# Mixture-of-experts kernel: every slot's rows gathered straight from the conditioned rows, without a table in slot order

## The reference

```python
def _L0_cond_ref(x, W, A, Bm, scalings, adapter_idx):
    H = jnp.einsum('btd,od->bto', x, W)
    xa = jnp.einsum('btd,brd->btr', x, A[adapter_idx])
    delta = jnp.einsum('btr,bor->bto', xa, Bm[adapter_idx])
    return H + delta * scalings[adapter_idx][:, None, None]
...
routing_weights = softmax_integer(xf @ w_gate.T)
top_w, top_i = jax.lax.top_k(routing_weights, 2)
top_w = top_w / top_w.sum(axis=-1, keepdims=True)
combine = jnp.zeros((T, E)).at[jnp.arange(T)[:, None], top_i].add(top_w)
for e in range(8):
    h = jax.nn.silu(xf @ w1[e].T) * (xf @ w3[e].T)
    out = out + combine[:, e:e + 1] * (h @ w2[e].T)
x = x + out
```

## Time and profile before

| | |
|---|---|
| median of 3 runs | 213.94 us |
| the three runs | 209.7, 213.94, 224.81 us |
| profiled execution: span from first to last instruction | 203.8 us |
| profiled execution's own time | not listed beside the runs; the fastest run, 209.7 us, is 5.9 us over the span |
| PE busy | 194.4 us (95%) |
| POOL busy | 134.7 us (66%) |
| DVE, ACT busy | 106.3 us (52%), 82.5 us (40%) |
| DMA traffic | 37.25 MB |

### The profile page before, as it was taken

How to read it: one execution, slowest core, us unless ns; L and a number is a source line. 1 busy time by engine, 2 the same in 40 slices (tenths; PEclk the granted TensorE clock), 3 DMA queues, 4 the chain that set the end, 5 groups by cost and what they waited for, 6 DMA issues and landing times.

```text
span 203.8 us, 3875 instructions
## 1 busy us (share of the span) xinstructions
PE 194.4 (95%) x1209; PEld 170.6 (84%) x1209; DVE 106.3 (52%) x307; ACT 82.5 (40%) x224; POOL 134.7 (66%) x115
## 2 busy tenths in 40 slices
PE   7799999699999999999999999999999999999992
PEld 6487998588778998899889988998889888988871
DVE  0568899683433454345334533453666344434484
ACT  2467484277653433243323332333234323432560
POOL 8300088787899968999999999999143474016600
PEclk9889999999999999999999999999999999999999
DMA  5999994499769993356436518202411121001915
GB/s 138 400 367 339 302 392 182 106 330 413 290 207 323 349 339 127 129 151 213 129 59 244 171 42 253 88 3 48 183 55 64 43 72 60 26 29 32 360 48 207
DMA packets 21634, 37.25 MB, mean 183 GB/s; under 512 B 2416, under 2 KB 14960, under 8 KB 21488
## 3 DMA queue, kind: packets, MB, share of 16 engines
q1 hardware_dynamic: 18080, 30.15, 44.8%
q0 software_dynamic: 1984, 5.25, 7.0%
q10 hardware_dynamic: 1552, 1.61, 2.4%
HBM read 25.45 MB, written 11.54 MB: 182 GB/s over the span
## 4 chain that ended last, share of the span: by engine, by line
PE 70%; POOL 9%; DMA 8%; ACT 4%; issue 4%; DVE 2%; SPq 0%; ACTq 0%; DVEq 0%; POOLq 0%
PE gu L1202 23%; PE gu L1211 11%; POOL slot_rows L490 7%; PE ya L1239 6%; PE ht L1218 6%; PE ya L1240 5%; PE ya L1241 5%; DMA x<-x_t 3%; DMA rows<-expert_rows 2%; ACT w_all L582 2%; PE xt L1182 2%; POOL rows L473 2%; DMA slot_rows<-c_rows,pos_i 2%; PE gu L1084 2%; DMA expert_rows<-rows,dst_i 1%
## 5 line engine op out<-in xcount | busy, mean ns | idle before, releaser
L1202 PE MATMUL gu<-w_all,xs_hi 128*128 (+2 forms) x276 | 70.8, 378 | 0.1
L902 DVE TENSOR_TENSOR hid<-gu,sg 128x256 f32<-128x256 f32 x46 | 19.5, 424 | 63.6 <-ACT sg L640 63.6
L1202 PEld LDWEIGHTS gu<-w_all,xs_hi 128*128 128x128 f32 x276 | 46.7, 188 | 4.5 <-issue 0.3
L479 POOL TENSOR_TENSOR w_all<-raw,w_all 128x1024 fp32r<-128x1024 f32 (+2 forms) x15 | 46.9, 3133 | 0.1
L640 ACT ACTIVATE sg<-gu 128x256 f32<-128x256 f32 x46 | 17.7, 384 | 70.5 <-PE gu L1211 70.5
L1211 PE MATMUL gu<-w_all,xs_lo 128*128 (+1 forms) x138 | 40.5, 374 | 0.0
L1239 PE MATMUL ya<-w_all,h_hi 128*128 (+1 forms) x115 | 38.5, 334 | 0.5 <-DVE h_lo L917 0.3
L509 POOL DMA_INDIRECT expert_rows<-rows,dst_i x21 | 20.6, 983 | 27.1 <-DVE rows L923 11.4
L490 POOL DMA_INDIRECT slot_rows<-c_rows,pos_i x16 | 19.3, 1207 | 23.3 <-DVE pos_i L825 18.7
L1240 PE MATMUL ya<-w_all,h_hi 128*128 (+1 forms) x115 | 32.5, 283 | 0.0
L1241 PE MATMUL ya<-w_all,h_lo 128*128 (+1 forms) x115 | 32.2, 280 | 0.0
(11 more groups left out here) (191 smaller groups left out, 268.5 us busy)
## 6 DMA issues: line engine op xcount, KB each, us to landing
raw<-expert_weights SPq DMA_DIRECT2D x6, 896.0 KB, 5.4
raw<-expert_weights SPq DMA_DIRECT2D x6, 640.0 KB, 5.6
raw<-expert_weights SPq DMA_DIRECT2D x6, 512.0 KB, 6.0
slot_rows<-zeros SPq DMA_DIRECT2D x1, 2432.0 KB, 16.4
expert_rows<-zeros SPq DMA_DIRECT2D x1, 2048.0 KB, 13.8
rows<-expert_rows SPq DMA_DIRECT2D x4, 512.0 KB, 5.4
rows<-slot_rows SPq DMA_DIRECT2D x1, 1152.0 KB, 8.3
cond_rows<-c_rows ACTq DMA_DIRECT2D x4, 256.0 KB
```

Source lines behind the costliest of these rows:

```text
L479: return nc.gpsimd.tensor_tensor(lo_part(e, cols), from_raw(e)[:, cols], as_f32(hi_part(e, cols)), ALU.subtract)
L902: nc.vector.tensor_tensor(hid[i % HBUFS][:, :].rearrange("p (a b) -> p a b", b=P), bank[:, :].rearrange("p (a k b) -> p a k b", k=2, b=P)[ ...
L1202: nc.tensor.matmul(out, stay_hi[:, kc * P:(kc + 1) * P], moving(at, part + first + kc * P, n), start=kc == 0 and part == HI_COLS, stop=False)
```

## The change

The table `slot_rows` is gone, with its zeros, the 16 sends, the four loads, `pos_i` and the semaphores for them. Slots 1 to 22 are all fetched by POOL's indirect DMA from `cond_rows`, one for each slot, in three runs: slots 1 to 5 behind `src_ready` (they lie outside `stage`; `CLEAR` is 6), slots 6 to 8 behind `low(2, ...)`, slots 9 to 22 behind `low(3, ...)`. Rows that belong to no token now hold token 0's row where they held zeros; their results go to spare rows as before. ACT's wait for the sends becomes one for `c_stored`. `destinations()` moves on DVE from step 5 to step 3, SP's zeros of `expert_rows` lose the loads ahead of them, and slot 4 is turned in step 1 of slot 3 (`LATE_SLOTS` loses it).

```diff
-GATHERED = 3
-EARLY_SENDS = 5
-LATE_SLOTS = (1, GATHERED + 1)
-
-FIRST_TILES = 4
-LOADED = [(GATHERED + 1, 6), (6, 10), (10, 14), (14, SLOTS)]
+LATE_SLOTS = (1,)
+
+
+CLEAR = SLOTS - HI_COLS // DIM
+FETCHED = {2: (CLEAR, 9), 3: (9, SLOTS)}
...
-            sp.wait_ge(zeros_ready, 1)
-            sp.dma_start(xs_dram[LOADED[0][0] * P:, :].rearrange("(p r) (h d) -> p (r h) d", p=P, h=KC),
-                         as_f32(zeros[:, :]).unsqueeze(1).broadcast_to(
-                             [P, (SLOTS - LOADED[0][0]) * KC, P])).then_inc(slots_zeroed, 16)
             raw_weights(1)
             raw_weights(2)
 
             sp.wait_ge(xt_done, 1)
             raw_weights(STAGED_LOW)
 
-            def slot_rows(g):
...
-            for i in range(2):
-                sp.wait_ge(c_sent[i], 16 * TOP * FIRST_TILES)
-            slot_rows(0)
-
+            sp.wait_ge(zeros_ready, 1)
             sp.wait_ge(w_ready, STAGED + 1)
-            for g in range(1, len(LOADED)):
-                slot_rows(g)
-
             sp.dma_start(y_dram[0:TOP * TOKENS, :].rearrange("(p r) (h d) -> p (r h) d", p=P, h=KC),
...
-            pool.wait_ge(pos_ready, 1)
-            pool.wait_ge(slots_zeroed, 16)
-            for n in range(EARLY_SENDS):
-                send(n)
             pool.wait_ge(src_ready, 1)
             pool.wait_ge(c_stored, 16 * (TILES // 2))
-            for s in range(1, GATHERED + 1):
+            for s in range(1, CLEAR):
                 gather(s)
-            for n in range(EARLY_SENDS, CHOICES):
-                send(n)
...
                 tail_low(e).then_inc(w_ready, 1)
+                for s in range(*FETCHED[e]):
+                    gather(s)
...
                 if 6 <= i < 9:
-                    if i > 6:
-
-                        act.wait_ge(c_sent[i - 7], 16 * TOP * FIRST_TILES)
+                    if i == 7:
+
+                        act.wait_ge(c_stored, 16 * (TILES // 2))
                     expert_hi(3, i - 6)
...
-            nc.vector.tensor_copy(pos_i[:, :], pos[:, :]).then_inc(pos_ready, 1)
...
-                if i == 5:
-                    destinations()
...
                 if i == 3:
+                    destinations()
                     expert_lo(1, 2)
                     expert_tail_lo(1).then_inc(w_ready, 1)
...
             def turn_slot(s):
-                if s <= GATHERED:
-                    pe.wait_ge(rows_in[s], 16)
-                for g, (first, _) in enumerate(LOADED):
-                    if s == first:
-                        pe.wait_ge(loaded[g], 16)
+                pe.wait_ge(rows_in[s], 16)
```

More of the change, by code:

```diff
@@ L107, in moe_kernel @@
     c_dram = nc.dram_tensor("cond_rows", (TOKENS, DIM), F32, kind="Internal").ap()
-    xs_dram = nc.dram_tensor("slot_rows", (SLOTS * P, DIM), F32, kind="Internal").ap()
     y_dram = nc.dram_tensor("expert_rows", (TOP * TOKENS + SLOTS * P, DIM), F32, kind="Internal").ap()
@@ L155, in moe_kernel @@
         pos = sb("pos", [P, CHOICES], U16)
-        pos_i = sb("pos_i", [P, CHOICES], U32)
         row_of = sb("row_of", [P, CHOICES], U16)
@@ L277, in moe_kernel @@
         slots_ready = sem("slots_ready")
-        pos_ready = sem("pos_ready")
-        slots_zeroed = sem("slots_zeroed")
-        c_sent = [sem(f"c_sent{i}") for i in range(2)]
-        rows_in = [sem(f"rows_in{s}") for s in range(GATHERED + 1)]
-        loaded = [sem(f"loaded{g}") for g in range(len(LOADED))]
+        rows_in = [sem(f"rows_in{s}") for s in range(SLOTS)]
         whi_ready = sem("whi_ready")
@@ L403, in _ @@
             raw_weights(STAGED_LOW)
-            def slot_rows(g):
-                first, stop = LOADED[g]
-                sp.dma_start(rows[:, first:stop, :],
-                             xs_dram[first * P:stop * P, :].rearrange("(s p) d -> p s d", p=P)).then_inc(loaded[g], 16)
-            for i in range(2):
-                sp.wait_ge(c_sent[i], 16 * TOP * FIRST_TILES)
-            slot_rows(0)
+            sp.wait_ge(zeros_ready, 1)
             sp.wait_ge(w_ready, STAGED + 1)
-            for g in range(1, len(LOADED)):
-                slot_rows(g)
             sp.dma_start(y_dram[0:TOP * TOKENS, :].rearrange("(p r) (h d) -> p (r h) d", p=P, h=KC),
@@ L484, in tail_low @@
                 return nc.gpsimd.tensor_tensor(stack, raw_tail(e, LOW_HALF), as_f32(stack), ALU.subtract)
-            def send(n):
-                t, k = n // TOP, n % TOP
-                j = k * TILES + t
-                pool.wait_ge(c_out, t // 2 + 1)
-                nc.gpsimd.indirect_dma_start(
-                    out=xs_dram[:, :], out_offset=bass.IndirectOffsetOnAxis(ap=pos_i[:, j:j + 1], axis=0),
-                    in_=c_rows[:, t, :], in_offset=None).then_inc(c_sent[t // FIRST_TILES], 16)
-            pool.wait_ge(pos_ready, 1)
-            pool.wait_ge(slots_zeroed, 16)
-            for n in range(EARLY_SENDS):
-                send(n)
             pool.wait_ge(src_ready, 1)
             pool.wait_ge(c_stored, 16 * (TILES // 2))
-            for s in range(1, GATHERED + 1):
+            for s in range(1, CLEAR):
                 gather(s)
-            for n in range(EARLY_SENDS, CHOICES):
-                send(n)
             def scatter(s):
```

## The result

The changed kernel took 216.06 us (median of 4 runs, 215.68 to 217.52), the kernel before 212.97 us (209.7, 212.01, 213.94, 224.81). A program can fall into a slower state of the chip, as the run of 224.81 did, so every ratio here is that of the fast runs alone, while the medians contain all runs. The ratio is 1.0245, 95% interval 1.020 to 1.029. The kernel is slower by about 2%, where 211.5 was forecast, 2.4 us less than the 213.94 of before. The profiled execution took 215.68 us with a span of 213.2, so 2.5 us lie around a span, and not the 5.9 that the forecast used.

What follows compares the result with a forecast made beforehand. PE was taken as the bound, busy for 95% of the span. An earlier first gather (0.9 us) and removed sends (1.5) sum to 2.4, other parts nothing: 213.94 - 2.4 = 211.5 us, range 206.3 to 216.5.

Steps and rivals of the forecast that it cites:

- the 5.9 that the forecast used: Time around the profiled span, suggested by the fastest run: 5.9 us, taking a span of 203.8 to 209.7.
- the row of 1.59: POOL's first gather in the profile before took 1.59 us, where a plain one takes 0.96.
- 85.7: Start of expert 4 on POOL behind the gathers of slots 9 to 22: 85.7 us, where it was 75.00.
- under 7.0: Sign that the forecast is right: slots 1 to 3 take under 7.0 us each.
- the forecast 34.05: First gather on POOL could start at 34.05 us instead of 34.91, 0.86 us sooner; 0.9 was taken.
- the forecast's 2.4: Total gain: 0.9 us from the earlier first gather plus 1.5 from removing the sends and ACT's wait for them.
- The slack is 8.6 us ... So POOL's delay is covered, at full.: Expert 5, needed by PE in slot 13, had 8.6 us of slack; experts 4, 6 and 7 had more.
- without this cover it would cost about 9.5 us: POOL's gathers ahead of expert 4 make experts 4 and 5 about 9.5 us later, the price if slack did not cover it.
- the 4.2 us between the fastest run and the median: The median shown, 213.94, was 4.2 us over the fastest run, without a reason in the profile; left in the forecast.
- POOL comes late with expert 5: Rival: DVE holds up 17 later gathers; slower from 0.65 us each, 222 us at 1.1 each; chance 0.06.
- More is won: Rival: slow transfers explain the median, so removing zeros, sends and loads wins up to 4.2 us more, 207.3; chance 0.18.

Runs made afterwards that it cites:

- second trace of the kernel before: The kernel before, run and profiled once more with nothing changed; median 212.53 us, ratio 1.002.
- pads spread: The changed kernel with each row that belongs to no token fetching a row of its own instead of token 0's; 217.40 us, ratio 1.023.
- cut up with pads spread: The changed kernel with padding reading its own rows and the third run of gathers split beside POOL's pieces of experts 4 to 7; 214.32 us.
- moves apart: The changed kernel with 8 gathers ahead of expert 7, the rest behind it, and late gathers and scatters taken apart; 208.18 us, ratio 0.981.
- held kernel: Slots 9 to 22 of the changed kernel filled by plain loads on SP, POOL then waiting until step 22 has its hidden units; 215.15 us.
- plain loads: The changed kernel with the third run's 14 gathers replaced by plain loads on SP's queue; 203.93 us, ratio 0.964.
- the late burst: The kernel with plain loads plus 14 gathers in a row after expert 7's weights, into places nobody reads; 220.26 us, ratio 1.036.
- cutting up the run: The changed kernel with slots 9 to 11 gathered behind expert 3, the others one by one beside POOL's pieces of experts 4 to 7; 214.16 us.

## Why the prediction was wrong

**Right.** The first gather started at 32.75, with no send ahead, and took 1.67 us, as the forecast took from the row of 1.59. PE's idle time before slot 1 fell from 1.76 to 1.00. Slots 2 and 3 took 6.91 and 6.81. POOL's schedule was right too: expert 4's first cast at 84.06 against 85.7, later gathers at 0.95 each. Slot 1 took 7.46, against my "under 7.0". PE waited 0.33 us of it behind DVE's copy of slot 0's result; `destinations()` now stands ahead of that copy, but the second trace of the kernel before has 0.75 us at the same place without it, so it can't be put down to that.

The gain by slot 6 was 3.3 us against 2.4, and the first gather started 1.3 us sooner than the forecast 34.05. About 1.0 us of both is luck. The stretch 8 to 13 us, before and after:

```profile
8.00:13.00 5.00, 4.98 (x22) 4.17 (x22) 3.90 (x8) 3.39 (x5) 0.00 (x0) 0.66 1.02 403
```
```profile
8.00:13.00 5.00, 4.55 (x28) 3.60 (x28) 3.87 (x9) 3.47 (x6) 0.00 (x0) 1.00 1.04 407
```

In the trace of before the granted clock was 0.5 for 3.4 us there, ahead of anything that was changed on PE, ACT or DVE, and ACT's last copy of conditioned rows began at 27.61 us where it begins at 26.60 now. The second trace of the kernel before has no such dip and its copy at 26.75; three traces of changed kernels have one in their first 17 us (pads spread, cut up with pads spread, moves apart). What is left of the gain, 2.3 us, is the forecast's 2.4.

**Wrong, first: "The slack is 8.6 us ... So POOL's delay is covered, at full."** The counts of rows per expert, on which this stood, were wrong. I had taken the two largest logits of each token; the reference rounds and clips them to integers first, and a tie goes to the lower expert. For the inputs as drawn this gives 369, 269, 241, 243, 191, 245, 230 and 260 rows; the experts end with slots 3, 6, 8, 10, 12, 14, 16 and 19, and the last four slots are spare. The held kernel shows it: experts 4 to 7 are wanted two slots apart. So POOL, at 16.5 us an expert, loses 2.8 us on each to PE's 13.7, and the slack shrinks from one to the next. With POOL's rows and these slots it was about 9.8, 7.1, 5.3 and 2.3 us before. A delay of 9.5 us is over all but the first, and PE's gain of 3.3 us takes more away. The forecast's price, "without this cover it would cost about 9.5 us", is near what was measured (held, POOL's lateness cost 10.7), but in part by chance. Expert 7 was complete at 149.83, 8.6 us later than before; less a slack of 2.3, plus the 3.3 that PE had gained, it came 9.7 us late, and the rest is lower clock behind PE's waits.

**Wrong, second: a term that was not in the sum.** This one made the changed kernel's time: its trace has no wait for `w_all`, and PE's 2.15, 1.01 and 5.17 us of idle time all stand in the third run of gathers or right behind it. POOL's gathers were counted by POOL's time and by their landing. That a row of them holds up PE's signals has no term; it cost 12 us here. The profile of before gave no row for it, because the execution in it had escaped; what it did give is the 4.2 us between the fastest run and the median, "for which the profile has no reason", and I carried them along as an offset. In the second trace, an execution of 212.08 us with a span of 210.0, it is this cost in the kernel before: it is 6.1 us behind the first trace by slot 3, right behind the sends, and hardly loses more. That the other runs at 211 to 214 us have the same reason is likely, but they were not looked into.

**The two do not add.** Lateness alone is 10.7 us over plain loads, the late burst 17.0, and the changed kernel, which has both, 11.2. In it the burst puts PE back by 12 us ahead of expert 4, and POOL's lateness hides behind that. This is why cutting up the run won only 2 us: it uncovered the other cost.

**The rivals.** "POOL comes late with expert 5", with 6 in 100, named the right engine and the wrong mechanism: it asked for hold-ups of 0.65 us per gather, of which there were none behind slot 5; the slack itself was missing. "More is won" (207.3) did not come; that slow transfers explain the spread of the runs, on which it stood, is not borne out by the second trace, where the time went with a late signal. What remains open is the path on which POOL's descriptors and the engines' signals meet. The runs show that it depends on the number of gathers and on the pause between them, and hardly on bytes; no run here looked inside it. Nor was it tried to free the kernel before of its burst, since its table can't be loaded until the last send has gone.

## What to carry to other kernels

Where two engines work at different paces, work out the slack at every hand-over, from the real data and the reference's own rounding, and not at the first; the last one is the tightest. Count indirect DMAs not only by the time of the engine that issues them: put work between them, though not so much that their rows come late, and check in the trace, signal by signal, that a consumer starts when its producer ends. A wait that is put down to "remote" or to an unknown queue on a kernel of one core is a finding, and a median over the profiled execution is a question to answer before the change is priced.
